# Coefficients of an attention step on VectorE instead of GpSimd, and an opening spread over five PSUM banks

## The reference: one transformer block with routed attention and a routed expert layer

```python
h = _layernorm(x) * (1 + ca) + sa
x = x + ga * attention(h)
h = _layernorm(x) * (1 + cb) + sb
x = x + gb * experts(h)
```

```python
tk_vals, tk_idx = jax.lax.top_k(logits, TOP_K)
tk_w = jax.nn.softmax(tk_vals, axis=-1)
for n in range(K_NODES):
    qr = q * c + _rotate_half(q) * s          # c, s: cosine, sine at the position in node n
    kr = k * c + _rotate_half(k) * s
    scores = jnp.einsum('bhid,bhjd->bhij', qr, kr) * SCALE
    scores = jnp.where(causal & mk, scores, NEG)
    outs.append(jnp.einsum('bhij,bhjd->bhid', softmax(scores), v))
y = (tk_w[..., None] * gathered).sum(axis=3)  # the two chosen nodes of each token
```

## Time and profile before

| | |
|---|---|
| median of 3 runs | 919.1 us |
| the profiled execution | 918.83 us, of which the span of the trace is 917.1 us |
| TensorE, VectorE, ScalarE, GpSimd busy | 826.5, 792.9, 733.0, 600.4 us (90, 86, 80, 65% of the span) |
| coef instructions on GpSimd (L560) | 256, together 53.0 us, 207 ns in the mean |
| TensorE's granted clock, mean | 0.981 |

### The profile page before, as it was taken

One profiled execution on the slowest core, in us unless ns is written; L12 is line 12 of the kernel. 1 busy time (PEld: TensorE's weight loads), 2 busy tenths in 40 slices (PEclk: granted clock), 3 DMA queues, 4 the chain that ended last, 5 costly groups with the idle time before them and its releaser, 6 DMA issues. The chain is left out here.

```text
span 917.1 us, 21368 instructions
## 1 busy us (share of the span) xinstructions
PE 826.5 (90%) x6552; PEld 580.4 (63%) x6552; DVE 792.9 (86%) x2003; ACT 733.0 (80%) x2001; POOL 600.4 (65%) x944
## 2 busy tenths in 40 slices
PE   4478989999999999999999999999999999999893
PEld 4456656666666666666666666666666666575793
DVE  6889978998899889988998899889988888777894
ACT  7268898889888988898889888988888887865572
POOL 4527768777877677767776777677656666127492
PEclk9699999999999999999999999999999999999997
DMA  9111111111211111111121111121101110323553
GB/s 219 32 18 30 37 31 43 37 36 25 43 41 37 24 41 39 38 29 37 36 41 30 39 37 36 32 41 31 14 9 16 16 14 13 127 70 93 153 166 113
DMA packets 81039, 45.01 MB, mean 49 GB/s; under 512 B 35072, under 2 KB 79808, under 8 KB 80928
## 3 DMA queue, kind: packets, MB, share of 16 engines
q1 hardware_dynamic: 79712, 41.15, 20.2%
q0 software_dynamic: 1216, 2.51, 0.8%
HBM read 30.62 MB, written 12.43 MB: 47 GB/s over the span
## 5 line engine op out<-in xcount | busy, mean ns | idle before, releaser
L1573 PE MATMUL psum<-QK 128*128 128x128 f32 (+3 forms) x1024 | 367.5, 451 | 2.3 <-ACT QK L740 1.8
L763 ACT ACTIVATE probs<-psum,negmax 128x128 f32<-128x128 f32 (+3 forms) x512 | 266.2, 527 | 48.6 <-DVE negmax L1157 32.5
L532 POOL TENSOR_TENSOR R<-pcs 128x512 f32<-128x512 f32 x126 | 172.7, 1392 | 59.7 <-DVE pcs L1088 59.7
L1573 PEld LDWEIGHTS psum<-QK 128*128 128x128 f32 x1024 | 158.3, 191 | 48.0 <-issue 41.8
L1168 DVE SCALAR_TENSOR_TENSOR accs<-probs,coef,accs 128x128 f32<-128x128 f32 (+3 forms) x256 | 164.7, 643 | 2.5 <-ACT accs L772 2.5
L772 ACT ACTIVATE accs<-probs,coef 128x128 f32<-128x128 f32 (+3 forms) x256 | 147.7, 577 | 23.4 <-POOL coef L560 23.2
L1088 DVE TENSOR_TENSOR pcs<-psum,arena 128x512 f32<-128x512 f32 x256 | 162.1, 674 | 1.7 <-POOL R L532 1.3
L560 POOL TENSOR_TENSOR coef<-rden,wslot 128x2 f32<-128x2 f32 x256 | 53.0, 207 | 167.9 <-DVE rden L1163 167.9
L1586 PE MATMUL psum<-ident,accs 128*128 128x128 f32 x640 | 115.9, 279 | 25.8 <-ACT QK L740 20.0
L1157 DVE CUSTOM_DVE_ANT_0 psum<-psum,outside 128x512 f32<-128x512 f32 x128 | 87.7, 700 | 51.4 <-PE psum L1575 50.7
L740 ACT ACTIVATE QK<-psum 128x384 f32<-128x384 f32 x235 | 115.6, 492 | 0.0
(11 more groups left out here) (278 smaller groups left out, 1560.9 us busy)
## 6 DMA issues: line engine op xcount, KB each, us to landing
weight_halves<-whl SPq DMA_DIRECT2D x48, 128.0 KB, 2.2
arena<-weight_halves SPq DMA_DIRECT2D x22, 256.0 KB, 3.1
wrow<-words SPq DMA_DIRECT2D x64, 86.0 KB
arena<-weight_halves SPq DMA_DIRECT2D x7, 512.0 KB, 6.8
wrow<-words SPq DMA_DIRECT2D x64, 42.0 KB
wst<-in_L_ffn_w_up_dram SPq DMA_DIRECT2D x14, 128.0 KB, 2.4
wst<-in_L_ffn_w_gate_dram SPq DMA_DIRECT2D x14, 128.0 KB, 2.4
wst<-in_L_ffn_w_down_dram SPq DMA_DIRECT2D x14, 128.0 KB, 2.4
```

Of the source, the lines that this page charges most:

```text
L532: pool.tensor_tensor(R[u][:, :, :, 0:3:2, half * HALF:(half + 1) * HALF].rearrange("p t e j f -> p (t e) j f"), halves(pc, half), halves(p ...
L763: act.activation((expB if e else expA)[:, k % (4 if e else 3), 0:w], area, ACT.Exp, scale=1.0 if k % TB < 2 else -1.0, bias=negmax[k % 4][ ...
L1573: pe.matmul(o, QK[:, u, e, rows], QK[:, u, 2, 0:w], start=True, stop=False)
```

## The change: where the coefficient is made, and how the opening is laid out

1. `coefficients` moves from GpSimd's list to VectorE's: the same 128x2 product of two SBUF tiles, now the last instruction of VectorE's step k (for step k - 1). GpSimd's loop keeps the rotations and splits and no longer waits for rden.
2. `products` of head 2 both stand in step 2 of VectorE (before: steps 1 and 2).
3. Opening: the transposed tiles of chosen rows get banks 0 to 3, the position tiles banks 4, 4, 6, 5; TensorE issues all of them ahead of the projection of head 1, and ScalarE empties them in that order. The load of the exponential's table moves behind the first `keep_qk`.
4. Opening: `dif * L` (128x1024) goes from VectorE to GpSimd.

```diff
+        def position_bank(b):
+            return bank[(4, 4, 6, 5)[b]]
...
-            def coefficients(k):
-                n, s = k // TB, k % TB
-                a = (n // H * TB + s) * H + n % H
-                if k == 0:
-                    pool.wait_ge(S["w_done"], 2)
-                pool.wait_ge(S["rden_done"], k + 1)
-                pool.tensor_tensor(coef[k % 4][:, :], rden[k % 4][:, :], wslot[:, a, :], ALU.mult
-                                   ).then_inc(S["coef_done"], 1)
-
+            pool.wait_ge(S["lg_ev"], 2)
+            pool.wait_ge(S["w_step"], 1)
+            pool.tensor_tensor(dif, dif, L, ALU.mult).then_inc(S["w_step"], 1)
...
-            for k in range(STEPS + 1):
+            for k in range(STEPS):
...
-                if k >= 1:
-                    coefficients(k - 1)
...
             trigonometry(0)
-            act.preload_act_table(ACT.Exp)
             keep_chosen(0, 0)
-            keep_positions(1)
             keep_chosen(1, 0)
-            keep_positions(2)
+            for b in range(1, B):
+                keep_positions(b)
             keep_chosen(0, 1)
-            keep_positions(3)
             keep_chosen(1, 1)
...
             keep_qk(0)
+            act.preload_act_table(ACT.Exp)
...
-            dve.wait_ge(S["w_step"], 1)
-            dve.tensor_tensor(dif, dif, L, ALU.mult).then_inc(S["w_step"], 1)
...
+            def coefficients(k):
+                n, s = k // TB, k % TB
+                a = (n // H * TB + s) * H + n % H
+                if k == 0:
+                    dve.wait_ge(S["w_done"], 2)
+                dve.wait_ge(S["rden_done"], k + 1)
+                dve.tensor_tensor(coef[k % 4][:, :], rden[k % 4][:, :], wslot[:, a, :], ALU.mult).then_inc(S["coef_done"], 1)
...
-                elif n == 0 and s < 3:
-                    products(2, s - 1)
-                elif s < 2 and n + 2 < NH:
+                elif k == 2:
+                    for e in range(2):
+                        products(2, e)
+                elif 0 < n < NH - 2 and s < 2:
                     products(n + 2, s)
+                if 1 <= k <= STEPS:
+                    coefficients(k - 1)
...
             position_rows(2)
+            position_rows(3)
+            chosen_rows(0, 1)
+            chosen_rows(1, 1)
             pe.wait_ge(S["prod_done"], 4)
             project(1)
-            chosen_rows(0, 1)
-            position_rows(3)
-            chosen_rows(1, 1)
```

More of the change, by code:

```diff
@@ L184, in block_kernel @@
         prod_cols = prod16.rearrange("p (t c n) -> p t c n", t=NT, n=NODES)
+        L = lg.rearrange("p (a n) -> p a n", n=NODES)
         dif = yT_flat[:, NS * NODES:2 * NS * NODES].rearrange("p (a n) -> p a n", n=NODES)
@@ L700, in keep_chosen @@
                 act.activation(mk[0:HD, half * 2:half * 2 + 2, 1 + e, :],
-                               bank16[(0, 0, 5, 0)[e + 2 * half]][0:HD, 0:2 * NEAR].rearrange("p (b t) -> p b t", b=2), ACT.Copy,
+                               bank16[e + 2 * half][0:HD, 0:2 * NEAR].rearrange("p (b t) -> p b t", b=2), ACT.Copy,
                                scale=BIG).then_inc(S["mk_ev"], 1)
@@ L705, in keep_positions @@
                 act.wait_ge(S["row_mm"], b + 1)
-                act.activation(posT[0:PIECED, b * T:(b + 1) * T], bank[4][0:PIECED, :], ACT.Copy, scale=1.0 / TURN
+                act.activation(posT[0:PIECED, b * T:(b + 1) * T], position_bank(b)[0:PIECED, :], ACT.Copy, scale=1.0 / TURN
                                ).then_inc(S["row_ev"], 1)
@@ L1001, in _ @@
             dve.wait_ge(S["lg_ev"], 2)
-            L = lg.rearrange("p (a n) -> p a n", n=NODES)
             M = member
@@ L1473, in chosen_rows @@
                 pe.wait_ge(S["sel_cp"], e + 1)
-                if half and not e:
-                    pe.wait_ge(S["words_done"], 1)
-                else:
-                    pe.wait_ge(S["mk_ev"], 4 + e + half)
+                pe.wait_ge(S["mk_ev"], 4)
+                if e + half:
+                    pe.wait_ge(S["trig_done"], TB)
+                    pe.wait_ge(S["ang_abs"], TB)
                 for t_ in range(B // 2 * (TB - 1)):
                     tile = (half * B // 2 + t_ // (TB - 1)) * TB + t_ % (TB - 1)
-                    mm_ = pe.transpose(bank16[(0, 0, 5, 0)[e + 2 * half]][0:HD, t_ * P:(t_ + 1) * P], sel16[:, e, tile * 64:(tile + 1) * 64],
+                    mm_ = pe.transpose(bank16[e + 2 * half][0:HD, t_ * P:(t_ + 1) * P], sel16[:, e, tile * 64:(tile + 1) * 64],
                                        ident16[:, :])
@@ L1497, in position_rows @@
                 if b:
-                    pe.wait_ge(S["row_ev"], b)
-                dst = bank[4]
+                    pe.wait_ge(S["row_ev"], 1)
+                if b == 2:
+                    pe.wait_ge(S["trig_done"], TB)
+                    pe.wait_ge(S["ang_abs"], TB)
+                if b == 3:
+                    pe.wait_ge(S["words_done"], 1)
+                dst = position_bank(b)
                 for tb in range(TB):
```

## The result

The changed kernel takes 964.2 us (median; 963.56 to 964.84), the kernel before 919.3 us beside it: a ratio of 1.049, with a 95% interval of [1.047, 1.051]. It is slower, as forecast, and by 45 us where 69 were forecast.

What follows compares the result with a forecast made beforehand. TensorE was taken to set the pace, VectorE close behind. Angle pairs 51.8, plain pairs 15.4 and table pairs 3.5 us, together 70.7, less 1.3 for the opening, on 918.8 gave 988 us; range 938 to 1015.

Steps and rivals of the forecast that it cites:

- 1.13 of waiting: Plain heads, second coefficient: held behind the second half of GpSimd's rotation part 0, so VectorE waits 1.13 us.
- the race in angle heads: Angle heads: GpSimd's L537 goes ahead of VectorE's `size_angles`; had VectorE's two instructions gone first, the head would pay 0.84 us.
- The angle pair: Even and odd angle head: 2 x 2.45 = 4.9 us, less 1.2 of waits, 3.7; times 14 is 51.8.
- the step said 1.7: Angle heads: `size_angles` and the coefficient wait for GpSimd's L537 and L540, so row maxima come 1.7 us later.
- the third: Third coefficient of a head, behind `place_outside`: held amid GpSimd's rotation; with `weigh_b`'s meetings and issue 0.6 us.
- The plain pair: Odd plain head's 1.9 us fit its 2.02 of waits, the even one's exceed 0.48 by 1.4; times 11 is 15.4.
- The price of 0.08: VectorE's list: one coefficient by itself adds 0.08 us, since short instructions overlap; 20 us for 256.
- Table pairs: Table heads: ScalarE's tables and sines cover VectorE's delay; 0.5 us kept for each of 7 pairs, 3.5.
- The opening's gain: Opening: head 0's transposes no longer wait behind the last copy of positions, so 1.3 us come back.
- Coefficients of 0.5 us in the mean: Sign in the profile: coefficients on VectorE, 0.17 us alone, would last 0.5 us or more in the mean.
- The two rivals that gave 903 and 918 us: 903: coefficient sooner, ScalarE's 14.8 us return, chance 0.08. 918: product free of GpSimd, VectorE without room, chance 0.05.
- the low end of 940: VectorE's pair goes ahead of L537: 7 us for angle pairs, 15.4 and 3.5 others, opening returns 4.5; chance 0.15.

Runs made afterwards that it cites:

- two_of_four: The changed kernel with the coefficients of steps 1 and 2 made by GpSimd again, steps 0 and 3 staying on VectorE: 929.0 us.
- rotation_in_halves: The changed kernel with every rotation instruction of GpSimd cut in two: 948.5 us.
- pool_paced: The changed kernel with GpSimd waiting for VectorE's reciprocal where it waited before the change: 939.6 us.
- one_input_paced: The changed kernel with each coefficient made by two 128x1 products of one tile and a scalar column, and GpSimd waiting for the reciprocal: 949.9 us.
- coef_early: The changed kernel with each coefficient issued right behind its reciprocal instead of last in VectorE's step: 979.2 us.
- early_and_gate: The changed kernel with each coefficient right behind its reciprocal and GpSimd waiting for the coefficient where it made it before: 963.5 us.
- short_masks: The changed kernel with the next head's two masks cut to 16 of 516 columns in some heads, so scores are not the kernel's: 957.9 us.
- one_input: The changed kernel with each coefficient made by two 128x1 products that take one tile and a scalar column: 957.2 us.

## Why the prediction was right, and where its sizes were off

**The mechanism held.** The products are held until GpSimd's instruction ends (1.04 us in step 1 of plain heads, where 1.13 of waiting was forecast), those of steps 0 and 3 are free (0.15 us lasting, 0.07 apart), `size_angles` lasts 1.19 us where over 1 was forecast, and of the 90.9 us that VectorE is busier the meetings make most: the 94 long products take 50.4 us beyond 0.15 each, `size_angles` takes 16.9 more and `weigh_b` 8.1, 75 us together. `two_of_four`, `rotation_in_halves` and `pool_paced` show that the time falls with them. The length of the list counts too: in `one_input_paced` neither products (0.20) nor `size_angles` (0.41) are held, and with two instructions for each coefficient it still stands 30 us above the kernel before. Of the race in angle heads, which no row had shown, the forecast's side came true: GpSimd's long instruction (L541) went ahead of `size_angles`, and its next one ahead of the product. `pool_paced` shows what pacing GpSimd is worth: 24.6 us, with `weigh_b`. The Trainium skill, "SBUF — State Buffer", section "Who interferes with whom", has the rule that two SBUF inputs and a GpSimd read exclude each other for a whole instruction, and that issue order decides; the products (1.04 us with two tiles, 0.20 with one) agree, and so does the order in angle head 16 (L541 at 262.75, `size_angles` at 263.22, L544 at 264.09, the product at 264.33).

**The angle pair was mis-sized: 3.7 us forecast.** A sum of 4.9 less 1.2 of waits; in the pair shown, VectorE's work grew by 4.16 and took up 1.30 of its idle time, net 2.86. The product behind `size_angles` costs 0.60 us (264.33 to 264.93), and `size_angles` 0.79 more than before (1.11 from its start to the next, against 0.32 in the earlier trace rows), 1.39 where the step said 1.7; the third costs 0.46 and `weigh_b` some 0.2 a head, where it said 0.6 for both. And not every pair pays: in heads 8 to 11 GpSimd has short instructions ahead of L541 when `size_angles` comes (in head 8 L494 with 0.76 us and L496 with 0.48); it then lasts 0.43 us, and the two pairs grow by 0.6 and 0.7. All 14 pairs, from first row maximum to first row maximum, add up to 33.9 us more, not 51.8.

**The plain pair was mis-sized: 1.4 forecast.** By the windows VectorE had 3.40 us idle in the pair, not the 2.5 that I added up from two waits, and got 2.71 more work, not 3.8. The price of 0.08 for a product right behind its reciprocal was too low as well (0.19). Ten of the eleven pairs pay 9.9 us, 1.0 each (the last has no next head to be cut at). Table pairs pay 0.2, not 0.5. The three kinds come to 45.2 us, where the sum said 70.7; head 0 starts 1.0 sooner, and what follows the first row maximum of head 62 takes 1.8 more.

**The opening's gain did not last.** The transposes start at 55.61, ahead of the 56.5 forecast, and head 0's row maxima 1.04 us earlier, close to the 1.3; `dif * L` took 2.38 us (estimate 2.1), hidden as said. But a step gained ahead of attention is not a step gained at its end: alone, it ended 2.4 us behind.

**Signs that were named.** Coefficients of 0.5 us in the mean: 0.35, since only 94 of 256 last over 0.25 us. VectorE's waits for scores below 20: 16.5. TensorE's busy share near 88%: 91%. GpSimd waits almost only for `products`: yes, 224.7 us. The two rivals that gave 903 and 918 us fall with the 89.0 us of the products; the low end of 940, VectorE winning the race, is near what `pool_paced` forces, at 939.6. That these two agree so well is luck: there the angle, plain and table pairs pay 13.1, 7.4 and 1.7 us, in the low end 7, 15.4 and 3.5, with 4.5 back from the opening.

**Open.** What lifts the times of `coef_early` and `early_and_gate` so far above their forecasts is shown in VectorE's busy time, and argued beyond it; why `weigh_b` is 15.8 us shorter in `pool_paced`; why the clock falls in some angle pairs and not in others with a standstill much alike; and the 2.4 us of the opening.

## What to carry to other kernels

Before moving a small instruction to a busy engine, read the windows cut at the work's own period: if the engine has no idle time in one class of periods, every microsecond there is paid, whatever its mean share says. Two SBUF tiles into VectorE beside a working GpSimd cost what is left of GpSimd's instruction, also for two elements, and so does an old instruction that now meets GpSimd at a new time: a wait that looks idle may be what keeps two engines apart. Here 128x1 products of one tile and a scalar column were not held, but masks of 128x16 in that form were. A product right behind the instruction that it depends on costs 0.1 us more.

## What the runs showed of the hardware that I had not expected

Tensor_scalars of VectorE with one SBUF tile behave differently beside GpSimd: `size_angles` (128x512) is held, as forecast, 1.19 us instead of 0.40, and so is a 128x16 mask of `short_masks`, 0.51 instead of 0.22, but the 128x1 of `one_input` is not, 0.20. GpSimd's instructions are lengthened in turn. L541 takes 1.38 us where `weigh_b` has 0.47 us left when it starts (head 16: 262.75, `weigh_b` until 263.22), and 1.05 in head 14; in `coef_early` it takes 1.38 us too, though `size_angles` starts only 1.3 us after it. Where `size_angles` is under way when it starts (`pool_paced`), it takes 1.15. And a standstill of TensorE of about 2 us in the middle of a pair of `short_masks` was followed by half the clock, at an estimate of 1.7 us, so that a stall of VectorE seems to be paid a second time there.
